# Twenty-eight whole tiles instead of sixteen, and the gathered rows turned by DMA transposes instead of on TensorE

## The chip, the cores and the metric

The kernel runs on one core of one Trainium2 chip. The metric is the device time of one execution in microseconds. Three executions of the kernel before took 536.46, 542.2 and 532.87 us; the median is 536.46. A profiled execution took 534.98 us, and its span in the trace is 533.0 us. All working below is made against that execution.

## The reference

The input is (4, 128, 32, 32): four images of 1024 positions with 128 channels. Three layers run one after the other, each with a residual:

```python
x = conv_attention(x)                       # softmax(theta^T phi) over 1024 positions, projected
t = to_tokens(x)                            # 4096 tokens of 128
t = t + attn(layernorm(t))                  # softmax attention per image
t = t + ffn(layernorm(t))                   # 8 experts, top 2, 128 -> 512 -> 128, exact gelu

def ffn(x):
    gate_logits = x @ Wg + bg
    top_w, top_i = top_k(gate_logits, 2);  top_w = softmax(top_w)
    w_dense = sum(one_hot(top_i) * top_w[..., None], axis=1)
    for e in range(8):
        h = gelu(x @ W1[e] + b1[e])
        out = out + w_dense[:, e:e+1] * (h @ W2[e] + b2[e])
```

The change touches only the last layer, the experts. 4096 tokens with two experts each make 8192 rows of work.

## The kernel before, in words

The two attention layers run first (until about 350 us). While the last image is in attention, the router of the earlier images is already done: VectorE ranks the tokens within their experts, and GpSimd writes each normalised token to `zbuf`, a buffer in HBM, at the place that its expert and rank give (64 indirect DMAs, L598). A row of `zbuf` holds 256 half-precision words (high and low parts of 128 values) and four that are two ids: where the result belongs.

Then come 36 tiles (`NT`). A **whole** tile is 256 rows of one expert; a tile of **halves** is two pieces of 128 rows, each with an expert of its own. Before, tiles 0 to 15 are whole (`FIRST` and `SECOND`, eight each, each from a list that VectorE builds), tiles 16 to 35 hold 39 halves (a third list). VectorE writes the lists and the experts of their entries to `tabi`, and counts them ready in `table_ready`.

A tile j goes through these steps:

- SyncE (SP) reads its place from the list and loads its rows into one of eight buffers `tin` (L490 whole, L496 for each half); for tile 8 and later it waits first until tile j-8 is finished (`y_ready`). Behind each of the loads of tiles 8 to 15 SP also issues two small transfers (`pad`, L479 and L480) that fill unused rows of `zbuf`.
- TensorE (PE) turns the rows with four transposes against an identity into a PSUM bank (`rows_T`, L1093), two tiles ahead; ScalarE (ACT) copies them to `zT` in SBUF (`rows_T`, L1204, EH<-PR).
- PE computes `hidden`: 12 matmuls of 256 columns for a whole tile, 24 of 128 columns for two halves, into one of two PSUM areas (SC for even tiles, PV for odd ones).
- ACT applies gelu (L1474) and copies the result to half precision (L1204, EH<-SC or EH<-PV); VectorE (DVE) makes the low halves (`low_halves`, L2025).
- PE computes `output` (MX<-QK,EH), behind the `hidden` of tile j+2 in its program.
- DVE makes the row addresses `yid` from the ids (L2035) and sums the output (L2039), which raises `y_ready`.
- GpSimd (POOL) writes the tile to `ybuf` in HBM with one indirect DMA for each half of 128 rows (`put`, L724).

At the end SP loads the results back from `ybuf` in pieces (L504), each when a certain count of tiles is written (`EARLY` = 28 for the first), DVE mixes the two results of each token into the residual (L2042, L2055), PE turns them, ACT moves them, and SP stores the output.

The order on each engine is the order of the code: the engines run their own programs and wait on semaphores. PE's program in the tile loop reads, for each j: `hidden(j)`, `output(j-2)`, `rows_T(j+2)`.

Of the kernel before, what the change touches and what calls it, by code (L numbers as in the profile page):

```python
# [55 lines left out]
WHOLE = FIRST + SECOND  # L56
# [3 lines left out]
EARLY = WHOLE + ((B - 1) * T * 2 + E - 1 - 2 * WHOLE + 1) // 2  # L60
# [6 lines left out]
def build(nc, x, theta_w, phi_w, proj_w, Wk, bk, Wq, bq, Wv, bv, Wg, bg, W1, b1, W2, b2, out):  # L67
    ds = bass.ds
    with ExitStack() as ctx:
# [86 lines left out]
        iotaj = sb("iotaj", [P, REST], F32)  # L156
# [3 lines left out]
        takes = sb("takes", [P, E], F32)  # L160
        upto = sb("upto", [P, E], F32)
# [19 lines left out]
        tin = EH0[:, 0:IN_BUFS * 2 * ROW].rearrange("p (b q r) -> p b q r", q=2, r=ROW)  # L181
        zT = EH0[:, IN_BUFS * 2 * ROW:IN_BUFS * 2 * ROW + 4 * TR].rearrange("p (b h r) -> p b h r", b=2, h=2)
# [92 lines left out]
        tin_full = [sem(f"tin_full{b}") for b in range(IN_BUFS)]  # L275
        zt_full = sem("zt_full")
        zt_ready = sem("zt_ready")
# [132 lines left out]
        def loads_of(j):  # L410

            return 16 * (min(j // IN_BUFS + 1, WHOLE // IN_BUFS) + 2 * max(0, j // IN_BUFS + 1 - WHOLE // IN_BUFS)
                         - (1 if len(halves(j)) == 1 else 0))
# [5 lines left out]
        def _(sp):  # L419
# [62 lines left out]
            def load_tile(j):  # L482

                b = j % IN_BUFS
                if j >= IN_BUFS:

                    sp.wait_ge(y_ready, j - IN_BUFS + 1)
                if j < WHOLE:
                    r = sp.value_load(tabi[0:1, 0, j:j + 1], min_val=0, max_val=E * CT - 1)
                    sp.dma_start(tin[:, b], zbuf[ds(r * TR, TR), :].rearrange("(q p) r -> p q r", q=2)) \  # L490
                        .then_inc(tin_full[b], 16)
                    return
                for q in halves(j):
                    k = listed_at(j, q)
                    r = sp.value_load(tabi[0:1, 0, k:k + 1], min_val=0, max_val=2 * E * CT + E - 1)
                    sp.dma_start(tin[:, b, q], zbuf[ds(r * P, P), :]).then_inc(tin_full[b], 16)  # L496
# [37 lines left out]
            for j in range(FIRST + SECOND, NT):  # L534
                load_tile(j)
            for k in range(2 * (B - 1)):

                written(EARLY + k)
                load_outputs(k, H * k, H)
# [9 lines left out]
        def _(pool):  # L549
# [16 lines left out]
            iot(iotaj[:], [[1, REST]], base=0, **kw).then_inc(iotas, 1)  # L566
# [166 lines left out]
        def _(pe):  # L733
# [349 lines left out]
            FT = [PR[:, h, :].bitcast(F16) for h in range(2)]  # L1083

            def rows_T(j):

                pe.wait_ge(tin_full[j % IN_BUFS], loads_of(j))
                if j >= 2:
                    pe.wait_ge(zt_ready, j - 1)
                for h in range(2):  # L1090
                    for q in halves(j):
                        at = h * TR + q * P
                        last = nc.tensor.transpose(FT[j % 2][:, at:at + P], tin[:, j % IN_BUFS, q, h * P:(h + 1) * P],  # L1093
                                                   ident16[:])
                last.then_inc(zt_full, 1)

            experts = [[pe.alloc_register(f"pe_expert{g}_{k}") for k in range(E)] for g in range(2)]

            def load_experts(g):

                pe.load(experts[g % 2], tabi[0:1, 1, E * g:E * (g + 1)])
# [6 lines left out]
            def hidden(j):  # L1108

                if j >= WHOLE and j % (E // 2) == 0:  # L1110
                    load_experts(listed_at(j, 0) // E)
                b = j % 2
                pe.wait_ge(zt_ready, j + 1)
                if j >= 2:
                    pe.wait_ge(hl_ready, j - 1)
                for q in (None,) if j < WHOLE else halves(j):
                    e = expert(j, q)
                    r = slice(0, TR) if q is None else slice(q * P, (q + 1) * P)
                    for c in range(HC):
                        o_ = WIDE[b][:, c * TR:(c + 1) * TR][:, r]  # L1120
                        w = ds(e * HID + c * P, P)
                        mm(o_, W1H[:, w], zT[:, b, 0, r], True, False)
                        mm(o_, W1H[:, w], zT[:, b, 1, r], False, False)
                        last = mm(o_, W1L[:, w], zT[:, b, 0, r], False, True)
                last.then_inc(h_full, 1)
# [26 lines left out]
            pe.wait_ge(pr_free[0], uses_before(UNITS + 2, 0) + 1)  # L1152
            rows_T(0)
# [4 lines left out]
            pe.wait_ge(pr_free[1], uses_before(UNITS + B - 1, 1) + 1)  # L1158
            pe.wait_ge(rank_read, 2)
            rows_T(1)  # L1160
            rows_T(2)
# [3 lines left out]
            rows_T(3)  # L1165

            for j in range(2, NT):
                if j == FIRST:
                    pe.wait_ge(table_ready, 4)
                    load_experts(1)  # L1170
                if j == WHOLE:
                    pe.wait_ge(table_ready, 6)
                hidden(j)
                if j == 2:
                    pe.wait_ge(last_logits_read, 1)
                    pe.wait_ge(wexp_lo, 2 * PAIRS)
                    pe.wait_ge(b2_ready, 1)
                    pe.wait_ge(picks_made, 2)
                if j == 3:
                    pe.wait_ge(rank_read, B)  # L1180
                output(j - 2)
                if j + 2 < NT:
                    rows_T(j + 2)
# [18 lines left out]
        def _(act):  # L1202
# [26 lines left out]

            FT = [PR[:, h, 0:TR].bitcast(F16) for h in range(2)]  # L1230

            def rows_T(j):
                act.wait_ge(zt_full, j + 1)
                r = slice(0, len(halves(j)) * P)
                cp(zT[:, j % 2, :, r], FT[j % 2].rearrange("p (h r) -> p h r", h=2)[:, :, r]).then_inc(zt_ready, 1)

            for s in STEPS:
# [166 lines left out]
                if s == UNITS + 1:  # L1404
                    rstds(*before)
                    rows_T(0)
                    normalise(*before)
                    turned()
                    continue
# [57 lines left out]
            rows_T(1)  # L1467
# [14 lines left out]
            for j in range(NT):  # L1482
                gelu(j)
                if j + 2 < NT:
                    rows_T(j + 2)
# [27 lines left out]
        def _(dve):  # L1513
# [171 lines left out]
            def not_done():  # L1685

                link(nc.vector.tensor_tensor(bases[:, 0:E], ecapt[:], done[:], ALU.add))
                link(nc.vector.tensor_tensor(tiles[:, 0:E], takes[:], done[:], ALU.subtract))

            def taken(n):  # L1690

                link(nc.vector.tensor_scalar(upto[:], ends[:, 0:E], float(n), None, ALU.min))
                nc.vector.tensor_tensor(takes[:, 1:E], upto[:, 1:E], upto[:, 0:E - 1], ALU.subtract)
                link(nc.vector.tensor_copy(takes[:, 0:1], upto[:, 0:1]))
                link(nc.vector.tensor_tensor(done[:], done[:], takes[:], ALU.add))

            def last_bases():

                link(nc.vector.scalar_tensor_tensor(out=bases[:, 0:E], in0=done[:], scalar=2.0, in1=ecaph[:],
                                                    op0=ALU.mult, op1=ALU.add))  # L1700
                link(nc.vector.tensor_tensor(bases[:, E:2 * E], ecaph[:], touched[:], ALU.add))
                link(nc.vector.scalar_tensor_tensor(out=tiles[:, 0:E], in0=done[:], scalar=-2.0, in1=touched[:],
                                                    op0=ALU.mult, op1=ALU.add))

            def last_tiles():

                counted_tiles(takes[:], ALU.is_gt, 0, P)
                link(nc.vector.tensor_tensor(tiles[:, E:2 * E], takes[:], touched[:], ALU.subtract))

            for s in STEPS:  # L1710
# [151 lines left out]
                def pair(i, before):  # L1862
# [50 lines left out]
                    if u == UNITS - 1 and i == PAIRS - 1:  # L1913
                        counted_tiles(takes[:], ALU.is_ge, TR, TR)
# [112 lines left out]
            def output(j):  # L2027
# [3 lines left out]
                words = tin[:, j % IN_BUFS, :, 2 * P:ROW].bitcast(I32)  # L2031
# [40 lines left out]
            counted_tiles(takes[:], ALU.is_ge, TR, TR)  # L2072
            counted_tiles(touched[:], ALU.is_gt, 0, P)
            logits_whole()
            tops(B - 1)
            picks(B - 1)
            for j in range(NT):
# [15 lines left out]
                if j == 3:  # L2093
                    taken(SECOND)
                    last_bases()
                if j == 4:
                    last_tiles()
                    segment_ends(2 * E)
                if j == 5:
                    segments_past(REST, 2 * E)  # L2100
                if j == 6:
                    segment_jumps(REST, 2 * E)
                if j == 7:
                    summed_past(FIRST + SECOND, REST, 2 * E)
                if j == 8:
                    summed_jumps(FIRST + SECOND, REST, 2 * E)
                    listed(FIRST + SECOND, REST, 2 * E)
# [35 lines left out]
```

## Time and profile before

| what | value |
|---|---|
| three executions, us | 536.46, 542.2, 532.87 (median 536.46) |
| profiled execution, us | 534.98 |
| its span, us | 533.0 |
| mean granted TensorE clock | 0.897 |
| PE busy | 405.6 us (76%) |
| DVE busy | 358.6 us (67%) |
| ACT busy | 332.0 us (62%) |
| POOL busy | 298.5 us (56%) |
| DMA queues, share of 16 engines | 14.1% (SP), 4.9% (POOL) |

No engine is busy all the time. The expert layer, the stretch that the change touches, is the last 40% of the span, and its engines take turns: what counts is the pace at which one tile follows another, and what sets it in each stretch. That pace is read from ACT, which starts exactly one gelu for each tile.

### The profile page before, as it was taken

What the parts mean: (1) busy time and instruction counts of PE and PEld (TensorE: products, weight loads), DVE (VectorE), ACT (ScalarE), POOL (GpSimd) and SP (SyncE); (2) the same over time, 40 slices, a digit from 0 to 9 for tenths busy, and PEclk for the clock granted to TensorE, in tenths of its full rate; (3) what the DMA queues carried; (4) which work ended last, traced back from release to release, by engine and by line L of the source; (5) the groups of instructions that cost most, each with busy time, mean ns of one, the idle gap of its engine ahead of it and who ended that gap; (6) DMA issues with size and microseconds to landing.
All of it is one profiled execution on the core that took longest, in us unless ns stands there. A gap on an engine that the chain in (4) does not pass through costs nothing. (4 is left out here: it accounts for less than half of the span.)

```text
span 533.0 us, 12741 instructions
## 1 busy us (share of the span) xinstructions
PE 405.6 (76%) x4063; PEld 293.6 (55%) x4063; DVE 358.6 (67%) x1008; ACT 332.0 (62%) x650; POOL 298.5 (56%) x304
## 2 busy tenths in 40 slices
PE   4777699989998999988856461572887789999824
PEld 3433476657676676755634350350776577777612
DVE  3786799978999898797578450650674355554556
ACT  5678678859787887766757131630675557665743
POOL 9235556776868665658837647057355345445430
PEclk9978999999999999998979785675799889999955
DMA  5041113000000000500101123011232212223445
GB/s 197 2 105 54 26 42 135 2 1 1 1 1 2 1 1 2 159 1 27 33 25 36 47 56 90 17 47 60 51 101 68 59 57 67 72 71 92 157 150 188
DMA packets 31969, 30.70 MB, mean 58 GB/s; under 512 B 8870, under 2 KB 25145, under 8 KB 31913
## 3 DMA queue, kind: packets, MB, share of 16 engines
q1 hardware_dynamic: 27594, 21.06, 14.1%
q0 software_dynamic: 4320, 8.92, 4.9%
q8 instruction: 33, 0.54, 0.4%
q14 instruction: 22, 0.18, 0.1%
HBM read 17.87 MB, written 12.08 MB: 56 GB/s over the span
## 5 line engine op out<-in xcount | busy, mean ns | idle before, releaser
L1293 ACT ACTIVATE E<-SC 128x512 f32<-128x512 f32 x128 | 77.1, 602 | 45.7 <-PE SC L735 42.7
L735 PE MATMUL PV<-VH,EH 128*128 128x129 f16 x512 | 96.5, 227 | 9.0 <-DVE TOK L1790 9.0
L735 PE MATMUL SC<-QK 128*128 128x512 f16 x326 | 92.9, 392 | 9.6 <-ACT EH L1294 3.4
L735 PE MATMUL PV<-VH,EL 128*128 128x129 f16 x512 | 96.3, 224 | 0.8 <-issue 0.8
L735 PE MATMUL PV<-VL,EH 128*128 128x128 f16 x512 | 96.2, 223 | 0.0
L598 POOL DMA_INDIRECT zbuf<-ZZ,posi x64 | 65.7, 1026 | 51.6 <-DVE posi L1633 34.0
L724 POOL DMA_INDIRECT ybuf<-EL,yid x55 | 54.2, 985 | 59.4 <-DVE EL L2039 48.7
L1748 DVE TENSOR_REDUCE mx<-MX 128x1 f32<-128x1024 f32 x56 | 68.2, 1217 | 19.8 <-PE MX L735 19.7
L1294 ACT ACTIVATE EH<-SC 128x512 f16<-128x512 f32 (+1 forms) x128 | 77.3, 604 | 0.0
L650 POOL TENSOR_TENSOR EL<-E,EH 128x1024 f16<-128x1024 f32 (+1 forms) x28 | 59.6, 2128 | 13.6 <-ACT EH L1294 13.4
L735 PE MATMUL MX<-QK,EH 128*128 x568 | 61.9, 255 | 6.1 <-issue 4.1
L735 PEld LDWEIGHTS PV<-VH,EH 128*128 128x128 f16 (+1 forms) x512 | 51.1, 100 | 15.8 <-issue 9.0
L735 PEld LDWEIGHTS MX<-QK,EH 128*128 128x128 f16 x568 | 47.5, 101 | 15.9 <-issue 10.3
L2025 DVE TENSOR_TENSOR EH<-PV,EH 128x1024 f16<-128x1024 f32 (+1 forms) x18 | 21.5, 1194 | 51.3 <-ACT EH L1204 51.2
L735 PEld LDWEIGHTS PV<-VL,EH 128*128 128x128 f16 (+1 forms) x512 | 52.0, 102 | 4.8 <-issue 0.3
L735 PEld LDWEIGHTS PV<-VH,EL 128*128 128x128 f16 (+1 forms) x512 | 50.8, 99 | 0.9 <-issue 0.9
L735 PEld LDWEIGHTS SC<-QK 128*128 128x128 f16 (+1 forms) x326 | 28.4, 100 | 33.8 <-issue 8.6
L735 PE MATMUL MX<-QK 128*128 128x512 f16 x122 | 38.4, 398 | 8.5 <-DVE mx L1748 5.9
L735 PE MATMUL SC<-EH,W1H 128*128 128x128 f16 (+1 forms) x224 | 34.0, 250 | 13.8 <-issue 12.4
L629 POOL TENSOR_TENSOR ZZ<-ZC,rstd 128x254 f16<-128x254 f32 (+1 forms) x24 | 14.6, 609 | 50.0 <-DVE rstd L1812 49.8
L1771 DVE TENSOR_TENSOR EL<-E,EH 128x1024 f16<-128x1024 f32 x28 | 38.2, 1363 | 6.6 <-ACT EH L1294 6.4
L2025 DVE TENSOR_TENSOR EH<-SC,EH 128x1024 f16<-128x1024 f32 x18 | 22.0, 1224 | 25.4 <-ACT EH L1204 15.9
(245 smaller groups left out, 910.6 us busy)
## 6 DMA issues: line engine op xcount, KB each, us to landing
EH<-zbuf SPq DMA_DIRECT2D x39, 65.0 KB
EH<-zbuf SPq DMA_DIRECT2D x16, 130.0 KB
X<-in_x_dram SPq DMA_DIRECT2D x4, 512.0 KB, 5.3
X<-in_L_ffn_W_dram SPq DMA_DIRECT2D x1, 2048.0 KB
EL<-ybuf SPq DMA_DIRECT2D x4, 512.0 KB, 3.9
out_dram<-X SPq DMA_DIRECT2D x8, 256.0 KB, 2.5
W1H<-in_L_ffn_W_dram SPq DMA_DIRECT2D x4, 256.0 KB, 4.5
W1L<-in_L_ffn_W_dram SPq DMA_DIRECT2D x4, 256.0 KB, 6.2
```

The costliest lines, as they stand in the source:

```text
L598: nc.gpsimd.indirect_dma_start(out=zbuf, out_offset=bass.IndirectOffsetOnAxis(ap=posi[:, q, t:t + 1], axis=0), in_=ZZ[:, t, :], in_offset= ...
L629: nc.gpsimd.tensor_tensor(ZZ[:, t, 1:P], ZC[:, :, 1:P], wide(rstd[:, a_ % 2, k], 1), ALU.mult)
L650: nc.gpsimd.tensor_tensor(EL[:, w % 2, ds(i * 2, 2), c], E32h[1], EH[:, w % 2, ds(i * 2, 2), c], ALU.subtract).then_inc(e32_free[1], 1)
L724: nc.gpsimd.indirect_dma_start(out=ybuf, out_offset=bass.IndirectOffsetOnAxis(ap=yid[:, b, q:q + 1], axis=0), in_=y32[b][:, q, :], in_offs ...
L735: return nc.tensor.matmul(o, w, r, start=start, stop=stop)
L1293: nc.scalar.activation(E32h[h][:, p, :], SC[:, p, :], ACT.Exp, scale=sc)
L1294: nc.scalar.activation(EH[:, x % 2, ds(i * 2 + p, 1), c], SC[:, p, :], ACT.Exp, scale=sc) \
L1748: nc.vector.reduce_max(mx[:, t:t + 1], MX[:], AX.X).then_inc(mx_free, 1)
L1771: nc.vector.tensor_tensor(EL[:, u % 2, ds(i * 2, 2), c], E32h[0], EH[:, u % 2, ds(i * 2, 2), c], ALU.subtract).then_inc(e32_free[0], 1)
L2025: nc.vector.tensor_tensor(low_, h_, high, ALU.subtract).then_inc(hl_ready, 1)
```

## The change

- **A third list of whole tiles.** Tiles 16 to 27 (`THIRD` = 12) are whole as well; the last list holds 15 halves in tiles 28 to 35 instead of 39 in tiles 16 to 35. The number of tiles stays 36. DVE builds the third list beside tiles 4 to 7 and the fourth beside tiles 9 to 12; `table_ready` goes to 8.
- **Turning by DMA.** `rows_T` is gone from PE and ACT. SP issues a DMA transpose from `zbuf` to `zT`, which now has eight buffers, and a second, small transfer for the ids. PE's `hidden` waits for the transpose (`zt_in`), DVE's `output` for the ids (`ids_in`).
- **Later first load of results.** `EARLY` is 32 instead of 28, and the following loads wait for 33, 34, 35, 36 and 36 tiles.
- PE loads the experts of the list to registers at tiles 8, 16, 24, 30 and 34 (before 8, 16, 20, 24, 28, 32).

The core of the diff (the rest are declarations, semaphores and the list arithmetic on DVE):

```diff
-WHOLE = FIRST + SECOND
+THIRD = (2 * TT - E) // 2 - FIRST - SECOND
+WHOLE = FIRST + SECOND + THIRD
 HALVES = 2 * TT + E - 1 - 2 * WHOLE
 REST = HALVES + HALVES % 2
 NT = WHOLE + REST // 2
-EARLY = WHOLE + ((B - 1) * T * 2 + E - 1 - 2 * WHOLE + 1) // 2
+EARLY = WHOLE + E // 2
...
-        tin = EH0[:, 0:IN_BUFS * 2 * ROW].rearrange("p (b q r) -> p b q r", q=2, r=ROW)
-        zT = EH0[:, IN_BUFS * 2 * ROW:IN_BUFS * 2 * ROW + 4 * TR].rearrange("p (b h r) -> p b h r", b=2, h=2)
+        zT = EH0[:, 0:IN_BUFS * 2 * TR].rearrange("p (b h r) -> p b h r", h=2, r=TR)
+        ids = sb("ids", [P, IN_BUFS, 2, 2], I32)
...
                 if j < WHOLE:
                     r = sp.value_load(tabi[0:1, 0, j:j + 1], min_val=0, max_val=E * CT - 1)
-                    sp.dma_start(tin[:, b], zbuf[ds(r * TR, TR), :].rearrange("(q p) r -> p q r", q=2)) \
-                        .then_inc(tin_full[b], 16)
+                    sp.dma_start_transpose(zT[:, b], zbuf[ds(r * TR, TR), 0:2 * P]).then_inc(zt_in[b], 16)
+                    sp.dma_start(ids[:, b].bitcast(F16),
+                                 zbuf[ds(r * TR, TR), 2 * P:ROW].rearrange("(q p) r -> p q r", q=2)) \
+                        .then_inc(ids_in[b], 16)
                     return
                 for q in halves(j):
...
-                    sp.dma_start(tin[:, b, q], zbuf[ds(r * P, P), :]).then_inc(tin_full[b], 16)
+                    sp.dma_start_transpose(zT[:, b, :, q * P:(q + 1) * P], zbuf[ds(r * P, P), 0:2 * P]) \
+                        .then_inc(zt_in[b], 16)
+                    sp.dma_start(ids[:, b, q].bitcast(F16), zbuf[ds(r * P, P), 2 * P:ROW]).then_inc(ids_in[b], 16)
...
-                written(EARLY + k)
+                written(min(EARLY + k, NT))
...
-                pe.wait_ge(zt_ready, j + 1)
+                pe.wait_ge(zt_in[j % IN_BUFS], loads_of(j))
...
                 output(j - 2)
-                if j + 2 < NT:
-                    rows_T(j + 2)
...
             for j in range(NT):
                 gelu(j)
-                if j + 2 < NT:
-                    rows_T(j + 2)
...
-                words = tin[:, j % IN_BUFS, :, 2 * P:ROW].bitcast(I32)
+                words = ids[:, j % IN_BUFS]
+                dve.wait_ge(ids_in[j % IN_BUFS], loads_of(j))
...
+                if j == 5:
+                    third_tiles()
                     segment_ends(2 * E)
...
+                if j == 10:
+                    last_halves()
+                    segment_ends(2 * E)
```

On SP, in the loads of tiles 8 to 15, one tile with its two filling transfers stands like this before (`tabi` is the list, EH holds `tin` and `zT`, `zer` and `padid` are what is filled in; the ISA rows work on registers):

```order
L489 TENSOR_LOAD tabi [waits y_ready]
L489 ISA x2
L490 ISA
L490 DMA EH<-zbuf 128x2x260
L477 TENSOR_LOAD padrow
L477 ISA x2
L479 ISA
L479 DMA zbuf<-zer 128x256
L480 ISA
L480 DMA zbuf<-padid 128x4
```

and like this in the changed program:

```order
L492 TENSOR_LOAD tabi [waits y_ready]
L492 ISA x2
L493 ISA
L493 DMA_TRANSPOSE EH<-zbuf 128x2x256
L494 ISA
L494 DMA ids<-zbuf 128x2x4
L480 TENSOR_LOAD padrow
L480 ISA x2
L482 ISA
L482 DMA zbuf<-zer 128x256
L483 ISA
L483 DMA zbuf<-padid 128x4
```

The plain load has become a transpose, and the transfer of the ids stands behind it; a half has the same pair, so a tile of two halves has four such transfers on SP.

On ACT, in the tile loop, three rows per tile before (L1474 gelu, L1204 EH<-SC or EH<-PV its copy to half precision, L1204 EH<-PR the turned rows of the tile two ahead):

```order
L1474 ACTIVATE PV<-PV 128x1024
L1204 ACTIVATE EH<-PV 128x1024
L1204 ACTIVATE EH<-PR 128x512
L1474 ACTIVATE SC<-SC 128x1024
L1204 ACTIVATE EH<-SC 128x1024
L1204 ACTIVATE EH<-PR 128x512
```

and two in the changed program (L1454 and L1193 are the same gelu and copy):

```order
L1454 ACTIVATE PV<-PV 128x1024
L1193 ACTIVATE EH<-PV 128x1024
L1454 ACTIVATE SC<-SC 128x1024
L1193 ACTIVATE EH<-SC 128x1024
L1454 ACTIVATE PV<-PV 128x1024
L1193 ACTIVATE EH<-PV 128x1024
```

The copy of the turned rows is gone; gelu and its copy stand back to back.

## Rows read from the trace of the kernel before

**Rows 1.** Windows: each engine's busy us (instructions), granted clock, DMA share.

```profile
core 0: us, PE busy (x) PEld busy (x) DVE busy (x) ACT busy (x) POOL busy (x), PEclk, DMA share, GB/s
...
407.00:440.00 33.00, 25.83 (x282) 21.62 (x283) 15.97 (x29) 17.93 (x23) 13.56 (x14) 0.90 0.21 59
440.00:500.00 60.00, 57.81 (x693) 45.27 (x691) 31.47 (x61) 38.20 (x46) 29.37 (x31) 1.00 0.29 86
```

**Rows 2.** Timeline of ACT (start, duration, what, idle before and its releaser).

```profile
375.41 1.02 ACT L1204 ACTIVATE EH<-PV 128x1024 f16<-128x1024 f32 x1 [5.52 <-remote]
...
376.80 1.03 ACT L1474 ACTIVATE SC<-SC 128x1024 f32<-128x1024 f32 x1
...
407.17 1.03 ACT L1474 ACTIVATE SC<-SC 128x1024 f32<-128x1024 f32 x1
...
439.63 1.01 ACT L1474 ACTIVATE PV<-PV 128x1024 f32<-128x1024 f32 x1 [1.02 <-PE PV L735]
...
499.11 1.01 ACT L1474 ACTIVATE SC<-SC 128x1024 f32<-128x1024 f32 x1 [1.54 <-PE SC L735]
```

**Rows 3.** Timeline of PE: a whole tile (from 408.32), a tile of halves (from 444.12).

```profile
408.32 0.39 PE L735 MATMUL PV<-EH,W1H 128*128 128x256 f16 x2 [1.70 <-DVE EH L2025]
...
409.63 0.71 PE L735 MATMUL MX<-QK,EH 128*128 x7
...
411.06 0.39 PE L1093 MATMUL PR<-ident,EH 128*128 128x128 f16 x4
...
444.12 0.38 PE L1093 MATMUL PR<-ident,EH 128*128 128x128 f16 x4
444.36 0.28 PE L735 MATMUL PV<-EH,W1H 128*128 128x128 f16 x2
...
446.48 0.72 PE L735 MATMUL MX<-QK,EH 128*128 x7
...
447.92 0.39 PE L1093 MATMUL PR<-ident,EH 128*128 128x128 f16 x4
```

**Rows 4.** Timeline of POOL: puts beside whole tiles, then beside halves.

```profile
409.05 0.97 POOL L724 DMA_INDIRECT ybuf<-EL,yid  x1 [4.17 <-DVE EL L2039]
...
412.88 0.96 POOL L724 DMA_INDIRECT ybuf<-EL,yid  x1 [0.30 <-issue]
...
447.96 0.97 POOL L724 DMA_INDIRECT ybuf<-QK,yid  x1 [1.64 <-DVE QK L2039]
```

**Rows 5.** Timelines of ACT and PE beside a run of four puts.

```profile
414.73 0.60 PE L735 MATMUL MX<-QK,EH 128*128 x6 [1.12 <-issue]
...
414.88 1.02 ACT L1204 ACTIVATE EH<-PV 128x1024 f16<-128x1024 f32 x1 [4.04 <-remote]
415.80 0.59 ACT L1204 ACTIVATE EH<-PR 128x512 f16<-128x512 f16 x1
```

**Rows 6.** Timeline of SP's queue: loads of tiles; time is that of issuing.

```profile
313.99 21.73 SPq L490 DMA_DIRECT2D EH<-zbuf  x8
...
396.83 0.33 SPq L490 DMA_DIRECT2D EH<-zbuf  x1
400.44 0.34 SPq L490 DMA_DIRECT2D EH<-zbuf  x1
...
448.51 1.51 SPq L496 DMA_DIRECT2D EH<-zbuf  x2
```

**Rows 7.** SP's loads of results, their landing (page part 6), and DVE's mixing.

```profile
487.34 15.63 SPq L504 DMA_DIRECT2D EL<-ybuf  x4
...
EL<-ybuf SPq DMA_DIRECT2D x4, 512.0 KB, 3.9
...
512.75 1.13 DVE L2042 SCALAR_TENSOR_TENSOR TOK<-EL,WT,TOK 128x128 f32<-128x128 f32 x4
```

**Rows 8.** Timeline of DVE: a small and a large step of building a list.

```profile
378.53 0.17 DVE L1693 TENSOR_TENSOR takes<-upto 128x7 f32<-128x7 f32 x1
...
385.34 0.81 DVE L1658 TENSOR_TENSOR W<-iotaj,ends 128x640 f32<-128x640 f32 x1
```

## What the change will do: the prediction

> **What bounds the kernel now.** I read the windows first, for the granted clock and for how full each engine is in each stretch; then ACT's timeline for the pace of the tiles; then PE, POOL and SP in one tile of each kind; last the tail.
>
> The windows show two stages that look alike in the code and are not alike in the trace [rows 1]. From 440 to 500 us, where tiles are halves, PE is busy 57.81 of 60 us at clock 1.00: it is the bound. From 407 to 440, where tiles are whole, it is busy 25.83 of 33 us, and no other engine is fuller.
>
> The gelu rows give the pace, one per tile [rows 2]. Tiles 4, 12, 19 and 34 start at 376.80, 407.17, 439.63 and 499.11: 3.80 us per tile from 4 to 12, 4.64 from 12 to 19 (16 to 18 are already halves), 3.97 from 19 to 34. So whole tiles, with less work for PE, are no faster than halves. PE's rows show how much less [rows 3]: a whole tile's hidden part takes 408.32 to 409.63, 1.31 us, a tile of halves 444.36 to 446.48, 2.12; the output part takes 1.43 in the one (409.63 to 411.06) and 1.44 in the other; turning the rows takes 0.24 (444.12 to 444.36). The halves' period on PE is 447.92 - 444.12 = 3.80, all of it work.
>
> What holds the whole tiles is seen by POOL's rows beside PE's and ACT's. POOL issues four puts of two tiles in one run, 409.05 to 412.88 + 0.96 = 413.84, with 0.30 between them, after 4.17 without work [rows 4]. ACT then waits 4.04 us, until 414.88, for something the trace only calls remote, and PE stands still for 1.12 until 414.73 [rows 5]: both go on about 1 us after the run of puts ended, not when a producer ended. I read this as: during a run of puts, the other engines' signals come late. It makes two tiles advance together, at 2 x 4.64 = 9.28 us per pair. In the halves POOL has 1.64 us without work before each pair of puts [rows 4], and the effect is gone; there PE sets the pace.
>
> **The change, part by part, tiles 4 to 34** (122.3 us before: 499.11 - 376.80).
>
> *Whole instead of half tiles.* Tiles 4 to 11 stay as they are: 8 x 3.80 = 30.4. Sixteen tiles (12 to 27) are now whole, four of them already before. If PE were the bound they would take 1.31 + 1.43 = 2.74 each; if they run as the whole tiles of before, 4.64 [rows 2, 3]. I lean to the second, because its cause stays and is nearer with a faster PE: a tile's two puts take POOL 2 x (0.97 + 0.30) = 2.54, so at 2.74 its pause would be 0.2 us, less than the 0.30 between the puts of a run and far from the 1.64 at which the effect is gone [rows 4].
>
> *The turned rows leave PE and ACT.* PE gains 0.24 per tile, ACT the copy of 0.59 [rows 3, 5]. In a whole tile's cycle of 9.28 ACT's two copies stand behind the held wait (415.80). If all of that was on the path, a tile takes (9.28 - 1.18) / 2 = 4.05; if none, 4.64. I take the middle, 4.35: 16 x 4.35 = 69.6. The ends for the range are 3.80, the pace of tiles 4 to 12, and 4.64. Six halves (28 to 34) at 3.97 are 23.8; PE's 0.24 could take them to 3.56, but then POOL's pause of 1.64 shrinks too, so I leave it. Sum 30.4 + 69.6 + 23.8 = 123.8, **+1.5**. Before tile 4, ACT was last held at 375.41 by the same remote wait, of 5.52 us, under the scatters [rows 2]; the turned rows were not what it waited for, so I cost that part at 0 (a gain of up to one tile, 3.8, is possible).
>
> *Transposes and ids on SP.* One transfer becomes two. The ids are a plain small transfer: its hold is that of a quiet load, 0.33 [rows 6]. The transpose is not in this trace. Its price T per issue is bounded by 0.33 (a quiet load) and 2.7 (the first eight loads, 21.73 / 8, beside the scatters) [rows 6]. Two halves took 1.51 together, thus one follows the other after 1.51 - 0.34 = 1.17, of it 0.84 not the transfer; now a half costs SP 0.84 + 0.33 + about 0.1 for the registers + T = 1.3 + T, and a whole tile the same. Loads run up to eight tiles ahead, so for whole tiles at 4.35 this stays hidden for any T up to 3.0. I take T near 0.5, since by tile 8 the scatters are over and the quiet rows are the nearest; cost 0. With 3.61 per load and its filling transfers (396.83 to 400.44) [rows 6] plus 0.34, SP has 3.95 in tiles 8 to 15: 0.15 over the pace of 3.80, for at most 1.2 us, taken by the lead.
>
> The Trainium skill, "VectorE: DVE Perf Modes", section "The three transpose paths", speaks against this edit: 1309 ns for a 128x128 tile by the DMA crossbar against 390 on TensorE, and the rule to use TensorE where a PSUM destination will do. By that, an estimate, a half's transpose takes 2.6 us and a whole tile's 5.2, SP could not keep up and the sum would be about 580. "DMA: Bandwidth & Descriptors", section "Latency and other measured facts", has 261 GB/s for such transfers, 0.5 us for a whole tile, and the sum would stay as it is. No row here decides between them.
>
> *Lists, registers, results.* DVE's list work grows by 27 instructions, between 0.17 and 0.81 each; the two large tables shrink from 640 columns to 192 and 256, so I count some 4 us over tiles 4 to 12, one step beside each tile [rows 8]. In the stretch behind it DVE is busy 15.97 of 33 us [rows 1]; cost 0, at most 4. PE's loads of experts go from six to five: 0.
>
> The first results were asked for at 487.34, when 28 tiles were written; now at 32, four tiles of 3.97 = 16 us later, about 503 [rows 7]. Six loads of 3.9 us land between 507 and 526 if one follows another, and mixing began at 512.75 [rows 7]. The early ones are still in time, the last ones no earlier than mixing would reach them: **+1.5**, ends 0 and +6.
>
> **Forecast M:** 534.98 + 1.5 + 1.5 = **538.0** us. This stands against the profiled execution; the median of the three is 1.5 higher, so against the median it is +0.3%. Its own range: 16 x 0.55 = -8.8 for whole tiles at 3.80, +4.6 at 4.64, tail -1.5 to +4.5: 527 to 547.
>
> **The rivals.**
>
> *A: the pairing breaks and PE becomes the bound.* For it: with the turned rows gone, hidden(j) no longer waits for ACT, which was what the held signals delayed; ACT keeps 1.03 + 1.02 = 2.05 us per tile [rows 2], POOL 2.54, both under PE's 2.74. Against it: POOL's pause of 0.2. Then tiles 4 to 11 take SP's 3.95, 31.6; sixteen take 2.74, 43.8; six halves 3.56, 21.4; sum 96.8, -25.5, +1.5 for the tail: **511**. If whole tiles take the halves' 3.56 instead, +13: 524.
>
> *B: the loads set the pace of the halves.* SP may begin tile 28's halves when tile 20 is finished; fifteen halves take it 15 x (1.3 + T), and PE gets from there to tile 35 in about 6 x 4.35 + 6 x 3.97 = 49.9. It decides from T = 2.0. At T = 2.7, 60.0: 10.1 late, **548**. If a whole tile's transpose takes twice that, 5.4, whole tiles fall behind too: 20 x 6.7 + 60 = 194 for SP against 20 x 4.35 + 8 x 3.97 = 119, of which a lead of some 30 is taken off: 45 late, about 583. For it: SP's issues do cost 2.7 where the queue is jammed [rows 6], and a transpose moves a row in other pieces than a plain load. Against it: beside tiles 8 and later the DMA engines are busy for 0.21 to 0.29 of the time alone [rows 1].
>
> *C: the pairing takes the halves as well.* PE without turning is 0.24 quicker per tile, POOL's pause shrinks, and runs of four never end: 22 x 4.64 + 30.4 = 132.5, +10.2, +1.5: **547**.
>
> **How the numbers follow.** M 0.38, A 0.30, B 0.20, C 0.12. A measurement of this kernel tells about 2% from no change (the three executions lie 1.7% apart): bounds 525.7 and 547.2. Faster is A: 0.30. Same is M and half of C, with a little of B's lower edge: 0.45. Slower is the rest of B and half of C: 0.25. The predicted time is M's, 538. The range is 513 to 550: below it lies A's lowest part (0.06), above it the worse half of B (0.12). M alone: 527 to 547.
>
> **What would show it.** In the changed trace: gelu starts of tiles 12 to 28 at 4.05 to 4.65 apart, in pairs, with runs of four puts and remote waits of some 4 us on ACT, mean M right; 2.7 to 3.6 apart and PE busy over 95% means A. SP's rows of transposes give T: over 2.0 for a half, with PE's waits released by SP's queue in tiles 28 to 35, means B; a few tenths and no such wait means my 0 was right. Gelu starts still in pairs after tile 28 mean C. The results' loads must land before DVE's mixing asks for them; a DVE wait there of over 3 us makes my tail wrong. I am wrong altogether if the time moved before tile 4, where I cost nothing, or if the transposes slow the puts or the loads of others.

## The result, and the profile after

Four executions of the changed kernel took 541.51, 546.09, 544.44 and 545.9 us, the median is 545.17; the kernel before, with a fourth execution of 529.98 beside the three, has 534.66. The quotient of these medians is 1.020; the estimated ratio is 1.0276, 95% interval 1.018 to 1.0373: slower, by 2.8%, though the interval reaches just below the 2% that was taken as the bound. The ratios in this document leave out executions more than 1.5% above the quickest of their kernel (of the whole tiles alone seven of twelve, of the kernel before in one batch five of seven), so they need not be the quotients of the medians. 545.17 lies inside the range of 513 to 550 and 7 us above the 538.0 forecast, which was made against the profiled execution; the one after is the quickest of its four, 541.51 with a span of 539.6, 6.6 more than before, and all stage times below are of those two.

Windows of the changed kernel (columns as in [rows 1]), one of whole tiles, one that still has whole tiles to 474.7, one of halves:

```profile
404.00:440.00 36.00, 25.43 (x245) 20.93 (x243) 18.73 (x36) 16.42 (x17) 15.96 (x17) 0.95 0.39 73
440.00:475.00 35.00, 27.66 (x252) 22.85 (x252) 15.26 (x25) 15.63 (x17) 15.54 (x16) 0.85 0.25 56
475.00:503.00 28.00, 22.99 (x247) 17.37 (x247) 11.90 (x21) 11.29 (x12) 11.64 (x12) 0.94 0.21 49
```

PE is busy 71%, 79% and 82%. The stretch of halves, which was full before (57.81 of 60 us [rows 1]), is no longer full.

ACT's gelu of tiles 4, 12, 28 and 34, the answer to [rows 2]:

```profile
374.44 1.02 ACT L1454 ACTIVATE SC<-SC 128x1024 f32<-128x1024 f32 x1
...
403.73 1.02 ACT L1454 ACTIVATE SC<-SC 128x1024 f32<-128x1024 f32 x1
...
474.67 1.02 ACT L1454 ACTIVATE SC<-SC 128x1024 f32<-128x1024 f32 x1
...
502.38 1.02 ACT L1193 ACTIVATE EH<-PV 128x1024 f16<-128x1024 f32 x1 [3.48 <-remote]
503.30 1.02 ACT L1454 ACTIVATE SC<-SC 128x1024 f32<-128x1024 f32 x1
```

The same count of tiles by stage, from the gelu starts of both kernels:

| stage | before, us | forecast M | after, us |
|---|---|---|---|
| start to tile 4 | 376.8 | no change | 374.4 |
| tiles 4 to 12 | 30.4 | 30.4 | 29.3 |
| tiles 12 to 28 | 67.4 | 69.6 (4.35 each) | 70.9 (4.43 each) |
| tiles 28 to 34 | 24.6 | 23.8 (3.97 each) | 28.6 (4.77 each) |
| tile 34 to the end | 33.9 | +1.5 | 36.3 |

In these two executions twelve more whole tiles are dearer than the halves they replace, and the halves that are left became dearer too. POOL's timeline in the halves, against [rows 4]:

```profile
496.58 0.97 POOL L734 DMA_INDIRECT ybuf<-EL,yid  x1 [4.58 <-DVE EL L2022]
497.86 0.97 POOL L734 DMA_INDIRECT ybuf<-EL,yid  x1 [0.30 <-issue]
499.13 0.97 POOL L734 DMA_INDIRECT ybuf<-EL,yid  x1 [0.30 <-issue]
500.41 0.97 POOL L734 DMA_INDIRECT ybuf<-EL,yid  x1 [0.31 <-issue]
505.80 0.97 POOL L734 DMA_INDIRECT ybuf<-EL,yid  x1 [4.42 <-DVE EL L2022]
```

Four puts in a run and 4.4 to 4.6 us without work: the pattern of the whole tiles has reached the halves, where pairs of puts with 1.64 us between them stood before. ACT's waits (what it waited for: us in total, times, longest) say the same. In the halves, first of the kernel before from 440 to 500 us, then of the changed one from 474 to 506:

```profile
ACT EH L1204 <- remote: 0.9, 2, 0.4
```

```profile
ACT EH L1193 <- remote: 11.7, 4, 3.5
```

From 404 to 475 us, where the kernel before has whole tiles and then halves and the changed one whole tiles only:

```profile
ACT EH L1204 <- remote: 12.3, 4, 4.0
```

```profile
ACT EH L1193 <- remote: 24.5, 7, 4.2
```

SP's queue, the transpose of the last whole tile and then two halves, against [rows 6]:

```profile
451.38 1.21 SPq L493 DMA_TRANSPOSE EH<-zbuf  x1
...
484.86 1.20 SPq L501 DMA_TRANSPOSE EH<-zbuf  x1
486.25 0.42 SPq L503 DMA_DIRECT2D ids<-zbuf  x1
487.42 1.21 SPq L501 DMA_TRANSPOSE EH<-zbuf  x1
488.82 0.43 SPq L503 DMA_DIRECT2D ids<-zbuf  x1
```

A half holds SP for 487.42 - 484.86 = 2.56 us, of it 1.20 for the transpose and 0.42 for the ids. PE's waits from 474 to 506 us, however, name no transfer at all:

```profile
PE SC L745 <- issue: 3.1, 7, 0.7
PE PV L745 <- DVE EH L2007: 3.1, 3, 1.3
```

So in this kernel the transposes arrive in time, and what PE waits for comes out of the chain of ACT and DVE. The tail: of DVE's waits from 515 to 532, those of the mixing for results:

```profile
DVE TOK L2025 <- DMA EL<-ybuf: 3.6, 2, 2.4
```

Before, from 512 to 526, DVE waited for no transfer there; the later loads of results cost 3.6 us of waiting, and the tail is 2.4 us longer.

### The profile page after: what moved, and what is told of

Same layout as the page of the kernel before. It is cut to its first block, busy times and chain, and to the rows that moved or that the text cites. A ratio compares the mean times of both kernels' runs of the same rounds, so it can differ in the third digit from the quotient of the medians.

```text
span 539.6 us, 11983 instructions
## 1 busy us (share of the span) xinstructions
PE 398.0 (74%) x3777; PEld 288.7 (54%) x3777; DVE 361.3 (67%) x1024; ACT 314.7 (58%) x614; POOL 299.8 (56%) x304
## 4 chain that ended last, share of the span: by engine, by line
PE 34%; DVE 22%; another core or an unknown queue 14%; ACT 11%; issue 9%; POOL 6%; DMA 2%; SPq 1%; ACTq 0%; POOLq 0%; DVEq 0%
PE PV L745 13%; PE SC L745 9%; PE MX L745 7%; PE PR L745 4%; DVE EH L2007 3%; POOL zbuf L608 3%; DVE mx L1730 3%; DVE EL L1753 3%; ACT EH L1193 3%; ACT PV L1454 2%; ACT EH L1276 1%; ACT E L1275 1%; ACT QK L1193 1%; DVE QK L1704 1%
## 5 line engine op out<-in xcount | busy, mean ns | idle before, releaser
L745 PE MATMUL PV<-VH,EH 128*128 128x129 f16 x512 | 99.5, 232 | 8.0 <-DVE TOK L1772 8.0
L745 PE MATMUL PV<-VH,EL 128*128 128x129 f16 x512 | 99.4, 229 | 0.0
L745 PE MATMUL PV<-VL,EH 128*128 128x128 f16 x512 | 99.3, 228 | 0.0
L745 PE MATMUL MX<-QK,EH 128*128 x568 | 68.0, 265 | 15.9 <-issue 14.0
L2007 DVE TENSOR_TENSOR EH<-PV,EH 128x1024 f16<-128x1024 f32 (+1 forms) x18 | 21.5, 1194 | 77.5 <-ACT EH L1193 70.4
L745 PEld LDWEIGHTS MX<-QK,EH 128*128 128x128 f16 x568 | 51.6, 105 | 27.2 <-issue 21.0
L745 PEld LDWEIGHTS PV<-VH,EH 128*128 128x128 f16 (+1 forms) x512 | 52.5, 103 | 14.5 <-issue 8.4
L745 PEld LDWEIGHTS PV<-VL,EH 128*128 128x128 f16 (+1 forms) x512 | 53.3, 104 | 5.1 <-issue 0.8
L745 PEld LDWEIGHTS PV<-VH,EL 128*128 128x128 f16 (+1 forms) x512 | 52.2, 102 | 0.3
L1193 ACT ACTIVATE EH<-PV 128x1024 f16<-128x1024 f32 (+1 forms) x18 | 18.0, 1001 | 58.2 <-remote 49.0
L745 PE MATMUL PV<-EH,W1H 128*128 128x256 f16 (+1 forms) x168 | 30.2, 284 | 20.8 <-DVE EH L2007 20.7
```

Of the source, the lines that this page charges most:

```text
L745: return nc.tensor.matmul(o, w, r, start=start, stop=stop)
L1193: return nc.scalar.activation(o, i_, ACT.Copy, scale=scale)
L2007: nc.vector.tensor_tensor(low_, h_, high, ALU.subtract).then_inc(hl_ready, 1)
```

## The experiments

All times are against the kernel before on the same chip. The stages come from the gelu starts of each profiled execution; the last column is ACT's wait from 404 to 475 us that the trace calls remote, for the copy to half precision. A wait of under 2 us for the same copy is mostly put down to PE in the trace and is not in this column.

Only with half the puts does the whole interval lie beyond 2%; of the other ratios the intervals tell the direction. The stages are of one execution each, and one kernel (the whole tiles alone) took 126.3 us for tiles 4 to 34 in one execution and 117.2 in another: smaller differences than that are not read from single rows without a cause seen in the trace.

| kernel | ratio (95%) | 12 to 16, us each | 16 to 28 | 28 to 34 | 4 to 34, us | after 34, us | remote, us |
|---|---|---|---|---|---|---|---|
| before | 1 | 4.58 | 4.09 | 4.09 | 122.3 | 33.9 | 12.3 |
| changed | 1.028 (1.018 to 1.037) | 4.38 | 4.45 | 4.77 | 128.9 | 36.3 | 24.5 |
| whole tiles alone | 0.979 (0.973 to 0.984), by medians 0.991 | 4.62 | 4.01 | 4.53 | 126.3 | 38.8 | 23.9 |
| transposes alone | 1.023 (1.016 to 1.030) | 4.49 | 4.95 | 5.42 | 142.2 | 34.5 | 18.9 |
| changed, half the puts | 0.961 (0.954 to 0.967) | 3.72 | 3.01 | 5.34 | 108.5 | 32.8 | 0 |
| changed, pause 0.51 | 1.014 (1.005 to 1.023) | 4.76 | 4.36 | 4.73 | 133.9 | 36.1 | 24.4 |
| changed, pause 0.94 | 0.985 (0.977 to 0.993) | 4.22 | 3.73 | 4.30 | 118.8 | 38.1 | 8.4 |
| changed, pause 1.37 | 0.984 (0.977 to 0.990) | 3.57 | 3.00 | 5.56 | 109.6 | 42.3 | 0 |
| whole tiles, pause 0.51 | 1.011 (1.004 to 1.018) | 4.35 | 4.06 | 4.57 | 127.6 | 39.8 | 21.5 |
| whole tiles, pause 0.94 | 0.981 (0.963 to 1.000) | 3.67 | 3.56 | 3.66 | 106.7 | 37.7 | 0 |
| whole tiles, pause 1.37 | 0.989 (0.985 to 0.993) | 3.10 | 3.03 | 3.79 | 97.2 | 55.7 | 0 |
| before, pause 1.37 | 0.976 (0.970 to 0.982) | 2.98 | 3.94 | 3.89 | 108.1 | 38.2 | 0 |
| before, pause 0.94 | 0.972 (0.960 to 0.984) | 3.20 | 3.93 | 4.08 | 109.9 | 30.0 | 0.4 |

My theory is P: a run of puts on POOL holds back PE's signals, and that sets the pace. Its rival is T: SP's transposes and second transfers do.

**Whole tiles alone.** The lists and tiles of the change on the kernel before; the rows are loaded plainly and turned on PE.

```diff
-WHOLE = FIRST + SECOND
+THIRD = (2 * TT - E) // 2 - FIRST - SECOND
+WHOLE = FIRST + SECOND + THIRD
...
                 pe.wait_ge(zt_ready, j + 1)
...
                 if j + 2 < NT:
                     rows_T(j + 2)
```

> The third list of whole tiles alone: the rows are still turned on PE and copied by ACT, SP loads plainly. Theory P (runs of four puts set the pace of whole tiles; the four lists decide): gelu starts of tiles 12 to 28 lie 4.4 to 4.7 us apart in pairs, tiles 4 to 34 take 126 to 131 us, and the time is that of the changed kernel, 1% to 3% above the kernel before. Theory T (the DMA transposes and the second transfer on SP's queue cost the time): with them gone the tiles take 120 us or less and the time is 0% to 2% below the kernel before.

Twelve executions took 525.96 to 543.11, median 535.16 against 540.05 before. The profiled one took 541.92: it shows P's pairs (126.3 us, remote waits of 23.9 us), with halves at 4.53 and no transpose in the program. So the pairs in the halves need no transposes. The time is T's: its median is 0.9% below the kernel before, where P had said 1% to 3% above. Without the transposes, then, the twelve more whole tiles do not make the kernel slower than before.

**The same once more.**

> The twenty-eight whole tiles without transposes and without a pause once more, since its executions lay far apart (525.96 to 543.11). If late signals come and go with the alignment of the pairs, an execution of about 527 shows runs of two puts and tiles 12 to 28 at 3.1 to 3.6 us each, one of about 540 shows runs of four at 4.2 to 4.7. If instead only the start before tile 4 or the tail differs, the gelu starts of tiles 4 to 34 take the same 126 us in both.

Four executions, 528.61 to 538.42, median 535.11 against 538.86 before. The profiled one (531.92) has tiles 16 to 28 at 3.54 and remote waits of 10.1 us, against 4.01 and 23.9 in the one of 541.92; tiles 4 to 34 took 117.2 against 126.3. In the halves it has runs of four puts as well, at 4.39 each. The pairs come and go within one program; what makes them set in is not settled by these runs. The four executions of the changed kernel lie together, at 541.51 to 546.09, and the trace of the quickest has pairs throughout. That the transposes make the pairs steady would fit, but is not shown: the two kernels were not run side by side.

**Transposes alone.** The 16 whole tiles and 39 halves of before, turned by DMA.

```diff
-                    sp.dma_start(tin[:, b, q], zbuf[ds(r * P, P), :]).then_inc(tin_full[b], 16)
+                    sp.dma_start_transpose(zT[:, b, :, q * P:(q + 1) * P], zbuf[ds(r * P, P), 0:2 * P]) \
+                        .then_inc(zt_in[b], 16)
+                    sp.dma_start(ids[:, b, q].bitcast(F16), zbuf[ds(r * P, P), 2 * P:ROW]).then_inc(ids_in[b], 16)
```

> The transposes alone: 16 whole tiles and 39 halves as before, but turned by DMA transposes with the small transfer of the ids. Theory P: PE loses 0.24 us of work per tile, its 39 halves keep 2.12 + 1.43 = 3.55 us of work per tile; either POOL keeps a pause of over 1 us between pairs and the tiles of halves go at 3.6 to 3.9 us (time 0% to 1.5% below the kernel before), or the runs of four spread into the halves and they go at 4.6 (time 1% to 2.5% above). Theory T: SP needs 2 x 2.55 = 5.1 us for a tile of two halves, so 20 such tiles end 15 to 25 us late, time 3% to 5% above, and PE waits for the transposes.

2.3% slower, tiles 4 to 34 19.9 us later, as T had said, though the time is under T's 3% to 5% and inside the 1% to 2.5% that P gave to runs of four. PE's waits from 430 to 520 us are mostly for the transposed rows:

```profile
PE PV L737 <- DMA EH<-zbuf: 11.0, 5, 3.0
PE SC L737 <- DMA EH<-zbuf: 5.1, 5, 1.5
```

Twenty tiles of two halves need 2 x 2.55 = 5.1 us each on SP, and go at 4.95 to 5.42. With fifteen halves, in the change, that is hidden; with thirty-nine it sets the pace. It is not alone: ACT still has 14.3 us of remote waits in the same stretch.

**The pause.** The changed kernel, with a memset of one row of scratch on POOL behind each tile's two puts.

```diff
                     nc.gpsimd.indirect_dma_start(
                         out=ybuf, out_offset=bass.IndirectOffsetOnAxis(ap=yid[:, b, q:q + 1], axis=0),
                         in_=y32[b][:, q, :], in_offset=None).then_inc(y_out[b], 16)
+                if j:
+                    pool.wait_ge(paused, j)
+                nc.gpsimd.memset(pause[0:1, :], 0.0).then_inc(paused, 1)
```

> The changed kernel with a pause of about 1.35 us on POOL (a memset of one row of scratch) behind the two puts of each tile. Theory P: runs of four are broken up although POOL has more to do; PE's signals come at most 1 us late, whole tiles go at POOL's 2.54 + 1.35 + 0.1 = 4.0 us each and no longer in pairs, tiles 4 to 34 take about 118 to 122 us instead of 128.9, the time falls by 1% to 2% against the changed kernel. If the puts are not what holds PE's signals, the pairs of tiles stay and more work on POOL changes nothing or adds up to 10 us.

More work on POOL made the kernel 1.6% faster than before, where without it it is 2.8% slower. POOL's timeline in the whole tiles:

```profile
430.79 0.97 POOL L736 DMA_INDIRECT ybuf<-EL,yid  x1 [0.17 <-issue]
432.07 0.97 POOL L736 DMA_INDIRECT ybuf<-EL,yid  x1 [0.30 <-issue]
433.03 1.37 POOL L741 MEMSET pause<- 1x1536 f16 x1
434.56 0.97 POOL L736 DMA_INDIRECT ybuf<-QK,yid  x1 [0.17 <-DVE QK L2027]
```

and the windows from tile 12 on:

```profile
404.00:452.00 48.00, 44.88 (x482) 38.91 (x481) 33.83 (x60) 30.72 (x31) 41.84 (x40) 1.00 0.39 79
452.00:485.00 33.00, 23.27 (x247) 17.69 (x245) 12.24 (x22) 11.84 (x12) 28.74 (x26) 0.93 0.26 59
```

PE is busy 94% of the whole tiles' stretch instead of 71%; tiles 16 to 28 go at 3.00, not at the 4.0 that I had expected of POOL (434.56 - 430.79 = 3.77 here), because results may wait in 24 buffers; tiles 4 to 34 take 109.6 us instead of the expected 118 to 122; and ACT has no remote wait left. But the halves go at 5.56: now PE reaches them early, and SP's 2.55 per half shows. PE's waits from 452 to 500 us:

```profile
PE PV L750 <- DMA EH<-zbuf: 3.6, 2, 2.0
...
PE SC L750 <- DMA EH<-zbuf: 2.0, 1, 2.0
```

**Half the puts.** Only the first put of each tile; half of the results are left out, the counts of puts that others wait for are halved with it, and zeros fill `ybuf` beforehand.

```diff
-                for q in halves(j):
+                for q in range(1):
                     nc.gpsimd.indirect_dma_start(
```

> The changed kernel with only the first put of each tile; the second half of each tile's results is left out, and the buffer in HBM is filled with zeros early on. Theory P: with 1.27 us of puts per tile in place of 2.54, a run for two tiles is 2.2 us long instead of 4.8, PE's signals are late by under 1 us, tiles 12 to 28 go at 2.7 to 3.3 us and tiles 4 to 34 take 95 to 110 us: 4% to 6% faster than the changed kernel. If something other than the puts holds the signals, tiles 12 to 28 stay at 4.2 to 4.7.

3.9% faster than before, tiles 16 to 28 at 3.01, no remote wait: this comes to the same without any added instruction on POOL, so it is the puts and not a side effect of the memset. The halves at 5.34 are again SP's, which I had not written down: PE's waits from 450 to 500 us have

```profile
PE SC L751 <- DMA EH<-zbuf: 3.9, 3, 1.7
PE PV L751 <- DMA EH<-zbuf: 3.6, 2, 2.5
```

**Whole tiles with the long pause.** Both causes gone (the edits are those above).

> Twenty-eight whole tiles with the rows turned on PE and copied by ACT as before, and the pause of 1.37 us on POOL behind each tile's puts. Theory P+S (runs of puts hold PE's signals; SP's transposes hold the halves): with both causes gone PE is the bound, 3.05 to 3.3 us for a whole tile and 3.8 for two halves, tiles 4 to 34 take 100 to 106 us; POOL needs 3.78 us per tile and ends late, about 505 us as in the run with transposes and the pause, so the tail is long and the time is 2% to 3.5% below the kernel before. If the halves stay at 5.3 us or more without transposes, SP's transposes were not what held them.

The pace is as expected or better: tiles 4 to 34 in 97.2 us, 25 less than before. The halves go at 3.79 without transposes, at 5.56 with them and the same pause: this is the control for SP's part. The windows of whole tiles and of the rest:

```profile
407.00:440.00 33.00, 32.70 (x375) 30.15 (x376) 24.76 (x47) 26.76 (x33) 28.74 (x27) 1.00 0.32 86
440.00:480.00 40.00, 39.32 (x472) 32.72 (x470) 22.06 (x38) 28.14 (x34) 35.08 (x33) 1.00 0.22 62
480.00:500.00 20.00, 3.58 (x43) 2.82 (x40) 4.99 (x13) 2.71 (x5) 17.52 (x16) 0.75 0.10 33
```

PE is full to 480 us and then waits for POOL, whose last put is this one:

```profile
510.37 0.98 POOL L733 DMA_INDIRECT ybuf<-EL,yid  x1 [0.17 <-issue]
```

The time is only 1.1% below the kernel before, not 2% to 3.5%: at 3.78 us per tile POOL is the bound, and the gain of rival A's pace (511 us) was lost again at the end, in a tail of 55.7 us.

**Shorter pauses.** 0.51 us with whole tiles and with the changed kernel, then 0.94 with whole tiles.

> The same with a short pause, about 0.46 us, so that POOL needs 3.0 us per tile and keeps up with PE. If a gap of 0.6 to 0.8 us between pairs of puts is enough to let PE's signals through, the tiles go as with the long pause (4 to 34 in 100 to 106 us), the tail is short again, and the time is 3% to 5% below the kernel before: the best version. If the gap must be longer, pairs of tiles with late signals come back and the time lies at that of the whole tiles without pause.

> The changed kernel with its transposes and the short pause. Against the long pause this tells what sets the end there: if the tail of 42 us is POOL's late puts (3.78 us per tile), the tail falls to 34 to 37 us and the time to 520 to 525; the halves stay at 5.1 to 5.6 us, since SP needs 2 x 2.55 us for two of them, whatever POOL does.

> Twenty-eight whole tiles, rows turned on PE, and a pause of about 0.9 us behind each tile's puts, between the 0.46 that left the pairs and the 1.37 that broke them. POOL needs 2.41 + 0.9 = 3.3 us per tile. If a gap of about 1.2 us between pairs of puts is enough: tiles 4 to 34 take 97 to 106 us as with the long pause, POOL's last put moves from 508 to about 491 to 495, the tail from 55.7 to 38 to 42, and the time is 3.5% to 5% below the kernel before, the best of all. If it is not enough, PE's signals are late by 2 to 4 us again and the time is that of the short pause, 1% above to 1% below the kernel before.

0.51 is not enough: 21.5 and 24.4 us of remote waits, times 1.1% and 1.4% above the kernel before; neither the tail of the one nor the halves of the other came as expected, since the pairs stayed. POOL there:

```profile
422.46 0.97 POOL L733 DMA_INDIRECT ybuf<-EL,yid  x1 [0.30 <-issue]
423.43 0.51 POOL L738 MEMSET pause<- 1x512 f16 x1
424.11 0.98 POOL L733 DMA_INDIRECT ybuf<-EL,yid  x1 [0.17 <-issue]
```

From the end of one put to the start of the next are 424.11 - 423.43 = 0.68 us. At a pause of 0.94 us, thus 1.1 between the pairs, whole tiles go at 3.56 and the halves at 3.66, the tail is 37.7, but 106.7 us in the tiles is just above what I gave, and 1.9%, with an interval that reaches no change, is less than my 3.5% to 5%. The column of remote waits, 0 here, hides why. ACT's and PE's rows of this kernel, then of the one with the long pause:

```profile
431.43 1.03 ACT L1488 ACTIVATE SC<-SC 128x1024 f32<-128x1024 f32 x1
...
434.10 1.01 ACT L1488 ACTIVATE PV<-PV 128x1024 f32<-128x1024 f32 x1
436.98 1.02 ACT L1218 ACTIVATE EH<-PV 128x1024 f16<-128x1024 f32 x1 [1.87 <-PE MX L747]
...
438.38 1.03 ACT L1488 ACTIVATE SC<-SC 128x1024 f32<-128x1024 f32 x1
...
435.22 0.27 PE L747 MATMUL MX<-QK,EH 128*128 x1
```

```profile
413.28 1.02 ACT L1218 ACTIVATE EH<-SC 128x1024 f16<-128x1024 f32 x1 [0.48 <-PE MX L747]
...
412.91 0.27 PE L747 MATMUL MX<-QK,EH 128*128 x1
```

The copy waits for the end of the output two tiles earlier. With the long pause it starts 413.28 - 413.18 = 0.10 us after PE's last row of that output, with the middle one 436.98 - 435.49 = 1.49, in every second tile from 409 to 458 us; the gelus still go in pairs, 2.67 and 4.28 apart. So 1.1 us between the puts makes the late signals shorter and does not end them.

**The kernel before with a pause,** 1.37 and 0.94 us.

> The kernel before with the long pause and nothing else. Tiles 12 to 19 fall from 4.6 to 3.1 to 3.8 us each, the tiles of halves stay at PE's 3.8; tiles 4 to 34 take 113 to 118 us instead of 122; POOL's 3.78 per tile is at PE's pace, so the tail stays within 3 us. The time is 0.5% to 2% below the kernel before. If it does not fall, the late signals cost nothing before and the reading of the whole tiles was wrong.

> The kernel before with the pause of about 0.9 us. With the long pause it was 2.4% below the kernel before, and its tail was 4 us longer than without. If the middle pause is enough, the tail is 2 to 4 us shorter and the time 2.5% to 3.5% below; if not, whole tiles 12 to 16 stay at 4.5 us each and the time within 1% of the kernel before.

2.4% and 2.8% faster, tiles 12 to 16 at 2.98 and 3.20 instead of 4.58, halves near PE's pace. With the long pause the tiles gained more than I had said (108.1 us, not 113 to 118) and the tail lost more (4.3 us, not under 3); with the middle pause the tail is 8.2 us shorter than that, not 2 to 4. The second, 516.81 us median against 538.86, is the best of these kernels that write all results. The late signals were costly before the change, too.

**The changed kernel with the middle pause.**

> The changed kernel, transposes and all, with the middle pause of 0.94 us; it differs from the whole tiles with the middle pause (tiles 4 to 34 in 106.7 us, 1.9% below the kernel before) only in how the rows are turned. If the transposes cost something of their own once PE's signals are less late: the tiles of halves 28 to 34 go at 5.1 to 5.6 us, where PE turning took 3.66, PE waits for transposes there, and tiles 4 to 34 take 113 to 118 us, time 0% to 1.5% below the kernel before. If they cost nothing, the halves go at 3.6 to 4.0 and the time is that of the kernel with PE turning or lower, 2% to 3% below.

1.5% below the kernel before, tiles 4 to 34 in 118.8 us, 12 more than with PE turning. But it does not tell the price of the transposes apart: the halves went at 4.30, not 5.1, PE waited for a transpose only once, 1.2 us, and 8.4 us of remote waits came back. The same pause leaves pairs with signals 1.5 us late when PE turns the rows, and waits of up to 4.2 us when it does not; why they are longer here is left open.

## Why the prediction was right, and where it was not

The number is in the range, partly by luck: the misses below add up to 10.5 us and cancel to 3.5. The direction was not the likeliest one: slower had 0.25, same 0.45.

**Whole tiles are tied to the runs of puts (forecast M): right.** 4.43 us each measured, 4.35 said. The pause and the half of the puts show the cause that I had only read from two rows: with the run broken or halved, they go at 3.0, PE's own pace with 2.74 of work.

**The halves keep 3.97: wrong, and the largest miss of the sum.** This step failed: "PE's 0.24 could take them to 3.56, but then POOL's pause of 1.64 shrinks too, so I leave it". The pause did not shrink a little; the runs of four went on and the halves took 4.77, 4.8 us more over six tiles. That is rival C, to which I gave 0.12, near its price of 4.64. The whole tiles alone showed 4.53 and 4.39 there without a transpose, so PE's 0.24 was not needed for it. M and C are one mechanism, and I should have asked where a run ends once it has begun: in the kernel before, it ended in the first halves (tiles 16 to 19); in the changed kernel and in the whole tiles alone it did not end in all the halves there are. What ends it is open.

**The transpose on SP costs 0: right for this kernel, for a wrong reason.** T was taken as 0.5 and is 1.2; the ids cost 0.43, not 0.33; a half 2.55 instead of 1.8. T stays under the 2.0 from which B was to decide, and PE waited for no transfer. But that 2.0 was worked out at 4.35 us per tile. At a pace of 3.0 the same 2.55 holds the halves, as two experiments and the control without transposes show, and A's 511 could not have been had with transposes: A took the halves at 3.56.

The Trainium skill, "VectorE: DVE Perf Modes", section "The three transpose paths", has 1309 ns for a 128x128 tile by the crossbar. The trace shows another thing, how long an issue holds SP's queue: 1.2, whether it turned two such tiles, for a half, or four, for a whole tile. Taken as a price per tile on that queue, the figure gave the estimate of 580, which did not come. The rule of the same page of the Trainium skill, section "Rules for kernel authors", to turn on TensorE where PSUM will do, agrees with two pairs of runs: with equal pauses tiles 4 to 34 took 97.2 and 106.7 us with PE turning, 109.6 and 118.8 with transposes.

**Tail +1.5: +2.4 measured,** with 3.6 us of DVE's waits for results; I had set a wait of over 3 as the sign that my tail is wrong, and so it is, by 0.9. **Before tile 4: -2.4,** inside the gain of up to 3.8 that I had left at 0, but I had also called a move there a sign of being wrong altogether. No cause was found for it: tile 4 starts at 374.4, 375.5, 375.9 and 376.5 us in the changed kernel without and with its three pauses, so most of the 2.4 is no more than executions differ by. Tiles 4 to 12, 1.1 quicker than said. The sum of the misses is +4.8 + 1.3 + 0.9 - 2.4 - 1.1 = 3.5, which takes 538.0 to 541.5, the profiled execution; the other 3.7 us up to the median of 545.17 stand in no trace.

## What to carry to other kernels

When a stage with less work is no faster, look at what its waits end with: here they ended with another engine's run of indirect DMAs; PE's saved work was lost in it, while 0.94 us of idle work between the puts made the kernel before 2.8% faster. Making the stage longer that moves in the rhythm of such a run spread the run to a stage that had been free of it. A transfer that is hidden at one pace has to be costed again at the pace that the change is meant to reach.

## What the runs showed of the hardware that was not expected

- With puts 0.30 us apart, PE's signals reached ACT 2 to 4 us late; with 0.68 us between pairs still; with 1.1 us they were 1.5 us late in every second whole tile of the twenty-eight where PE turns the rows, and ACT waited up to 4.2 where it does not; with 1.5 us they came mostly 0.1 to 0.4 us after PE's last row. Whether POOL's issuing or the transfers that it starts hold them, and which path they share, is not shown by any run here.
- A DMA transpose held SP's queue for 1.2 us in most rows, for 128 rows as for 256, a plain load of 256 rows for 0.33.
